# State-space block of a decoder: the read-outs of three pairs of states are added on GpSimd before TensorE sums them

## The reference, cut to what matters

```python
xz = x @ W_in                                   # x is the layer-normed input
x_in, z = jnp.split(xz, 2, axis=-1)
xc = silu(conv4(x_in) @ pw_kernel + conv_bias)
x_dbl = xc @ W_x                                # 16 delta ranks, 8 B, 8 C
delta = softplus(delta @ W_dt + b_dt)
deltaA = exp(delta * A)                         # per channel and state n
deltaB_u = delta * Bm * xc
def step(h, inp):
    dA_t, dBu_t, C_t = inp
    h = dA_t * h + dBu_t
    y_t = jnp.einsum('bn,bdn->bd', C_t, h)      # sum over the 8 states
    return (h, y_t)
y = y + xc * D
y = y * silu(z)
return y @ W_out
```

## Time and profile before

| | us |
|---|---|
| median of 3 runs | 3070.16 |
| the profiled execution, its own time | 3073.5 |
| its span, first to last instruction | 3071.7 |
| the 8 groups of this block, first scan to last finish (104.85 to 774.05) | 669.20 |
| one group in the middle of the block | about 85.0 |
| of it PE busy / DVE busy / ACT busy / POOL busy | 79.5 / 72.3 / 52.8 / 3.0 |

### The profile page before, as it was taken

One profiled execution on the slowest core, in us unless ns is written; L12 is line 12 of the kernel. 1 busy time (PEld: TensorE's weight loads), 2 busy tenths in 40 slices (PEclk: granted clock), 3 DMA queues, 4 the chain that ended last, 5 costly groups with the idle time before them and its releaser, 6 DMA issues. The chain is left out here.

```text
span 3071.7 us, 60127 instructions
## 1 busy us (share of the span) xinstructions
PE 2722.0 (89%) x20702; PEld 1767.6 (58%) x20703; DVE 1997.4 (65%) x4542; ACT 1518.1 (49%) x2982; POOL 454.4 (15%) x482
## 2 busy tenths in 40 slices
PE   6899999996799999999876689999999799969993
PEld 3344444443466676766665347777777645556662
DVE  2588888888367777777555447777777555653334
ACT  2666666663156666666443136666666233302222
POOL 0000000000300000000033111000110032324441
PEclk9899999997899999999877789999999899969997
DMA  4000000000100000000000100000000120001225
GB/s 112 0 1 0 0 0 0 0 0 0 35 21 20 20 15 20 20 20 15 1 15 1 39 11 26 20 20 20 20 25 11 49 83 20 14 26 61 63 61 165
DMA packets 57938, 80.70 MB, mean 26 GB/s; under 512 B 8880, under 2 KB 47059, under 8 KB 57491
## 3 DMA queue, kind: packets, MB, share of 16 engines
q1 hardware_dynamic: 51778, 62.69, 7.2%
q0 software_dynamic: 6048, 16.52, 1.7%
HBM read 63.59 MB, written 15.60 MB: 26 GB/s over the span
## 5 line engine op out<-in xcount | busy, mean ns | idle before, releaser
L1120 DVE CUSTOM_DVE_ANT_0 xa_h_scores<-xa_h_score_bank,xa_h_added 112x375 f32<-112x375 f32 x1024 | 518.1, 544 | 148.5 <-PE xa_h_score_bank L1055 133.6
L1214 ACT ACTIVATE xa_h_probs<-xa_h_scores,xa_h_negmax 112x375 f32<-112x375 f32 x1024 | 561.4, 600 | 0.9 <-DVE xa_h_negmax L1127 0.6
L1067 PEld LDWEIGHTS xa_h_turn_bank<-keep_ident,xa_h_probs 112*125 112x125 f32 x3072 | 398.6, 190 | 91.4 <-DVE xa_h_probs_t L1134 22.2
L1067 PE MATMUL xa_h_turn_bank<-keep_ident,xa_h_probs 112*125 112x112 f32 x3072 | 438.5, 279 | 8.8 <-DVE xa_h_probs_t L1134 8.5
L1134 DVE COPY xa_h_probs_t<-xa_h_turn_bank 125x448 f32<-125x448 f32 x512 | 319.1, 623 | 150.9 <-PE xa_h_turn_bank L1067 137.6
L1220 ACT ACTIVATE xa_h_probs_t<-xa_h_turn_bank 125x448 f32<-125x448 f32 x256 | 138.6, 541 | 304.5 <-PE xa_h_turn_bank L1067 304.5
L464 PE MATMUL mb_y_bank<-mb_read_out,keep_ident 128*128 128x448 f32 x512 | 231.7, 601 | 30.3 <-DVE mb_read_out L671 30.3
L664 DVE TENSOR_TENSOR_SCAN mb_state<-mb_decay,mb_drive 128x1792 f32<-128x1792 f32 x64 | 253.8, 3965 | 0.2 <-ACT mb_decay L598 0.2
L1055 PE MATMUL xa_h_score_bank<-xa_h_keys,xa_h_queries 32*112 32x375 f32 x2048 | 231.6, 522 | 11.3 <-DVE xa_h_row_max L1120 10.7
L1080 PEld LDWEIGHTS xa_h_sums_bank<-xa_h_probs_t,xa_h_values 125*32 125x32 f32 x6144 | 141.9, 110 | 154.5 <-DVE xa_h_probs_t L1134 149.2
L1080 PE MATMUL xa_h_sums_bank<-xa_h_probs_t,xa_h_values 125*32 125x112 f32 x6144 | 202.7, 265 | 14.6 <-issue 7.3
(11 more groups left out here) (341 smaller groups left out, 4145.7 us busy)
## 6 DMA issues: line engine op xcount, KB each, us to landing
xa_context<-in_ctx_t SPq DMA_DIRECT2D x64, 375.0 KB, 3.1
lm_w<-in_m_w SPq DMA_DIRECT2D x16, 512.0 KB, 9.9
lm_e_wide<-lm_result_rows SPq DMA_DIRECT2D x8, 896.0 KB, 9.8
keep_x<-in_x SPq DMA_DIRECT2D x4, 896.0 KB, 16.0
lm_latent_rows<-lm_rows SPq DMA_DIRECT2D x8, 448.0 KB, 3.2
out_x<-keep_x SPq DMA_DIRECT2D x8, 448.0 KB, 6.3
xa_mask_raw<-in_key_mask SPq DMA_DIRECT2D x1, 1312.5 KB
mb_f_pw<-in_pw SPq DMA_DIRECT2D x1, 1024.0 KB
```

Source lines behind the costliest of these rows:

```text
L1067: last = pe.transpose(turn_bank[(par + kc) % 2][0:KP, g * S:(g + 1) * S], probs[par][:, g, kc * KP:(kc + 1) * KP], keep.ident[0:S, 0:S])
L1120: dve.tensor_tensor_reduce(scores[par][:, g, :], score_bank[g][0:S, 0:SK], added[s][:, :], 1.0, -BIG, ALU.add, ALU.max, row_max[par][:, g: ...
L1214: act.activation(probs[par][:, g, :], scores[par][:, g, :], ACT.Exp, bias=negmax[s][:, G * c + g:G * c + g + 1]).then_inc(probs_ready, 1)
```

## The change

Three pairs of read-outs, of states 0 and 1, 2 and 3, 4 and 5, are added by POOL in SBUF (`add_pair`), and PE pushes the sum once, one state later (at n = 2, 4 and 6). States 6 and 7 are pushed singly as before. So a group has 5 pushes (20 matmuls) where it had 8 (32 matmuls), and 3 POOL additions of 128 x 1792 where it had none. The read-out tile has three buffers where it had two; `BUFFER` says in which one each state's read-out goes, `SUM` in which one POOL writes each sum (over one of its inputs). The read-outs of states 3, 5 and 7 now wait for POOL's additions, those of 4 and 6 for pushes. `skip` moves from state 0 to behind the first `convolve` in state 1. The pair additions stand ahead of `split_low` in POOL's queue.

```diff
--- before.py
+++ after.py
@@ -313,7 +313,7 @@
         delta, delta_inner = sb("delta", [128, IC, T]), sb("delta_inner", [128, IC, T])
         decay = sb("decay", [128, 2, IC, G, S])
         drive, state = sb("drive", [128, 2, IC, T]), sb("state", [128, 2, IC, T])
-        read_out = sb("read_out", [128, 2, IC, T])
+        read_out = sb("read_out", [128, 3, IC, T])
         gated_y = sb("gated_y", [128, IC, T])
         y_bank = [psum(f"y_bank{n}", [128, 512]) for n in range(IC)]
         front_bank = [psum(f"front_bank{n}", [128, 512]) for n in range(2)]
@@ -331,6 +331,11 @@
         decay_ready, drive_ready, state_ready, read_out_ready, summed = (
             sem(n) for n in ("decay_ready", "drive_ready", "state_ready", "read_out_ready", "summed"))
         skipped, gated, x_added = sem("skipped"), sem("gated"), sem("x_added")
+        pair_ready = sem("pair_ready")
+        PAIRS = 3
+        PUSHES = N - PAIRS
+        BUFFER = (0, 1, 2, 0, 1, 2, 0, 2)
+        SUM = (1, 0, 1)
         LOADED = mamba_w.count
 
         def slots(g):
@@ -381,7 +386,15 @@
                 pool.wait_ge(parts_cast, 2 * g + 2)
                 pool.tensor_tensor(low_parts[0:LOW, :], rest[0:LOW, :], low_parts[0:LOW, :], ALU.subtract).then_inc(split, 1)
 
+            def add_pair(g, k):
+
+                pool.wait_ge(read_out_ready, N * g + 2 * k + 2)
+                pool.tensor_tensor(read_out[:, SUM[k], :, :], read_out[:, BUFFER[2 * k], :, :], read_out[:, BUFFER[2 * k + 1], :, :],
+                                   ALU.add).then_inc(pair_ready, 1)
+
             def group(g, at, final=False):
+                for k in range(PAIRS):
+                    add_pair(g, k)
                 if not final:
                     split_low(g + 1)
 
@@ -458,11 +471,19 @@
                     last = pe.matmul(y_bank[c][:, 0:T], skip_diag[:, c, :], inner[:, c, :], start=True, stop=False)
                 last.then_inc(skipped, 1)
 
-            def add_state(g, n):
+            def push(held, stop):
+
+                for c in range(IC):
+                    last = pe.matmul(y_bank[c][:, 0:T], keep.ident[:, :], read_out[:, held, c, :], start=False, stop=stop)
+                last.then_inc(summed, 1)
+
+            def push_pair(g, k):
+                pe.wait_ge(pair_ready, PAIRS * g + k + 1)
+                push(SUM[k], False)
+
+            def push_state(g, n):
                 pe.wait_ge(read_out_ready, N * g + n + 1)
-                for c in range(IC):
-                    last = pe.matmul(y_bank[c][:, 0:T], keep.ident[:, :], read_out[:, n % 2, c, :], start=False, stop=n == N - 1)
-                last.then_inc(summed, 1)
+                push(BUFFER[n], n == N - 1)
 
             def project_out(g, half):
 
@@ -491,9 +512,10 @@
                         gate(g)
                         if not final:
                             turn_rows(g)
-                        skip(g)
                     if 1 <= n < 5 and not final:
                         convolve(g, n - 1)
+                    if n == 1:
+                        skip(g)
                     if n == 5:
                         if not final:
                             low_rank(g)
@@ -505,7 +527,10 @@
                             pe.wait_ge(split, 2 * (g + 2))
                             spread(g + 1, 0)
                         project_out(g, 1) if not first else pass_over(OUT_B)
-                    add_state(g, n)
+                    if n in (2, 4, 6):
+                        push_pair(g, n // 2 - 1)
+                    if n >= 2 * PAIRS:
+                        push_state(g, n)
 
             pe.wait_ge(loaded, LOADED)
             pe.wait_ge(setup, 1)
@@ -666,13 +691,16 @@
 
             def make_read_out(g, n):
                 dve.wait_ge(row_read[1], use_of_row(g, 1, n) + 1)
-                reuse(dve, summed, N * g + n - 1)
+                if n in (3, 5, 7):
+                    reuse(dve, pair_ready, PAIRS * g + n // 2)
+                else:
+                    reuse(dve, summed, PUSHES * g + {0: -1, 1: -2, 2: 0, 4: 1, 6: 2}[n])
                 dve.wait_ge(state_ready, N * g + n + 1)
-                dve.tensor_tensor(read_out[:, n % 2, :, :], state[:, n % 2, :, :],
+                dve.tensor_tensor(read_out[:, BUFFER[n], :, :], state[:, n % 2, :, :],
                                   rows[:, n % 2, 1, :].unsqueeze(1).broadcast_to([128, IC, T]), ALU.mult).then_inc(read_out_ready, 1)
 
             def finish(g):
-                dve.wait_ge(summed, N * (g + 1))
+                dve.wait_ge(summed, PUSHES * (g + 1))
                 dve.wait_ge(front_read[(GATES + 2) % 2], used(g, GATES + 2) + 1)
                 dve.wait_ge(front_read[(GATES + 3) % 2], used(g, GATES + 3) + 1)
                 for c in range(IC):
```

## The result

The changed kernel takes 3061.65 us (median of 9 executions, 3060.19 to 3069.17) against 3070.16 (9, 3064.97 to 3073.68) for the kernel before: ratio 0.9979, 95% interval 0.9970 to 0.9989. Run again on another occasion it gave 0.9977 (0.9966 to 0.9988). I had forecast 3073, a loss of 3 us that could not be told from none. The time lies in my range, but it went the other way, by just over the 0.2% that I had set as the bound.

A forecast was written before the change was run, and what follows sets the result against it. PE was taken to bound mid-group, with turn-taking at both ends. DVE's 568.4 us plus additions 92.4, cover -4.2, heads 6.4 + 4.4 and closing 5.0 gave a 672.4 us block, +3.2, hence 3073 us; range 3050 to 3100.

The forecast's parts named there:

- The bounds and the removal: Middle of a group: PE sets the pace at 9.4 us per state; three pushes fewer save it 9.0 us per group.
- the 1.64 us gaps: DVE's idle time before the drive of a next state, waiting for rows; forecast to go.
- The stall of DVE: Each POOL addition, 4.05 us, stops DVE for nearly its length: 3.85 us, 24 times, 92.4 us.
- The cover by `add_to_x`: Third addition runs beside `add_to_x` (input in PSUM), sparing DVE 0.6 us in seven groups, 4.2 in all.
- Rival 1: Additions cost DVE less than their length, 2.97 us each: 21 us less, 3052; chance 0.12.
- rival 2: POOL and DVE run side by side over long instructions, without blocking: 85 us less, 2985; chance 0.06.
- The heads: Group starts, where engines take turns: DVE's 3.58 us wait becomes 1.5 to 1.6 in four slow-gate groups, 6.4 us.
- The first group's wait: Head of the first group: DVE free at 116.4, rows at 120.8, so a wait of 4.4 us.
- The closing waits: End of the last group: DVE's waits for the last projection and last push, kept at 5.0 us.
- The sum for the block: All eight groups: DVE work, additions, cover, heads and closing waits give 672.4 us against 669.2, +3.2.
- Rival 3: PE at the lower clock makes rows late; drives of state 4 or 6 wait about 4 us: 3101; chance 0.20.
- The chances: Whole kernel against the one before: faster 0.27, same 0.34, slower 0.39.

The follow-up runs named there:

- half_additions: Changed kernel with each POOL addition over only the first two of four chunks (128x896 instead of 128x1792); ratio 0.9819 to the kernel before.
- after_padded: Changed kernel with 189 counting PE instructions ahead of PE's first wait for weights, restoring PE's old program length; ratio 1.0044 to the kernel before.
- after_again: Changed kernel run again with nothing altered; ratio 0.9977 to the kernel before, 3060.1 us in its profile.
- one_pair: Changed kernel with PAIRS = 1: only states 0 and 1 are added on POOL, 7 pushes a group; 3051.15 us, ratio 0.9936 to the kernel before.
- one_late_pair: Changed kernel with only states 4 and 5 added, pushed at state 6, and skip kept in state 0; ratio 0.9985 to the kernel before.
- memset_instead: Changed kernel with POOL filling the tile by a 128x1792 memset in place of each addition; ratio 0.9759 to the kernel before.
- No_additions: Changed kernel without the 24 POOL additions, each pair's push taking the second read-out alone; 3003.34 us, ratio 0.9772 to the kernel before.

## Why the prediction was wrong, and where it was right

**The bounds and the removal.** Right. PE set the pace in the middle, and the 1.64 us gaps went.

**The stall of DVE.** Right in mechanism and nearly in size: 3.71 us for 3.85, seen as drives of 5.74 us where I had said about 5.9. The half length gave half the stall (half_additions). The cover by `add_to_x` is right to the tenth, 3.71 - 3.11 = 0.6. Rival 1, the cheaper addition, is refuted by these rows, and rival 2 as well.

**The heads.** Mis-sized: I took 1.6 us per slow head, it is 2.6 (3.58 before), because PE's gates there run at the lower clock for 6.15 us where they took 4.97. The first group's wait is 4.2 for 4.4. The closing waits are 1.84 + 1.53 = 3.4, not 5.0. PE is busy 74.5 us in a middle group, where I had said 65 to 72, for the same reason: it runs the gates and some pushes at the lower clock.

**The sum for the block.** 672.4 forecast, 669.4 and 669.5 measured; a middle group 84.9 forecast, 85.3 measured. Against three profiles of the kernel before in which the block's code is its own (669.2, 665.6 and 665.6 with padding) the block is 0.2 to 3.9 us longer, which holds the forecast of +3.2. Part of that is luck, for the terms erred in both directions: the additions came 3 us cheaper (85 us for 88), the closing waits 1.6 shorter, the heads 4 dearer. And after_padded, with the same work, took 660.5. Rival 3 did not come: the second pair push of the third group does start late and at the lower clock (4.97 us), but the drives of states 4 and 6 never waited.

**The step that failed** is one I did not write as a step at all: that the block's change is the kernel's. I put the sum "on the profiled execution's 3073.5" as if the other 2300 us were fixed. They were not. The change moved PE's code, and with it a gap left the latent attention, 5 us, shown by padding either kernel. That term alone turns +3 into -2. In the two first profiles, whose spans differ by 6.9 us, it is nearly all: -0.4 us ahead of the block, +0.2 in it, -0.6 in the cross-attentions, -5.1 in the latent attention, -1.0 in the rest. The medians differ by 8.5 us and the ratio stands for 6.5. Beyond the 5 I find two things. One goes with the clock that the first cross-attention is granted: 6.8 us between two profiles of the changed kernel, in three stretches, 3.0 of it in the one at 0.88 or 0.62. The other is the 3 us that the changed kernel needs less behind that stretch in both profiles, without a known cause. If all nine of the shorter executions are like after_again, 6.4 us shorter behind the block, that is worth 9/16 x 6.4 = 3.6 us in the mean, and -2 becomes -5 to -6. That is an estimate: only one of the nine was profiled. What decides which clock is granted, and whether the change brings it about, stays open.

**The chances.** 0.27 on faster was low in the light of the result, but nothing in my rows priced the term that decided. That the time fell inside my range is owed to the range's width; its centre had the wrong sign.

## What to carry to other kernels

An addition moved to GpSimd is not free for VectorE where both read two SBUF inputs: price it as VectorE time of the addition's own length, and move only as much as VectorE's gaps will hold. Here one pair of three was right (3051 against 3062 and 3070). Where a forecast is a few us in 3000, pad the program of the old kernel to the new length before believing a gain: a change of nothing but code length was worth 5 us here. It is a test of what can move, not a correction, since two programs of one length (one_pair, one_late_pair) differed in the same gap. And when a cost is taken away, look at who gets the turn it leaves: without the additions POOL's split waited behind three DVE instructions, and the late softplus took back 28 us.

## What the runs showed of the hardware that I had not expected

- The place of PE's code decides about a gap of 3.5 to 4.3 us in a loop a long way behind the edit, and with it goes the number of fetch packets (71 with the gap, 61 or 62 without). Two programs 16,384 bytes apart behaved alike; two of equal length did not.
- 189 PE instructions that only count up a semaphore moved PE's first matmul from 12.35 to 32.10 us and the block by 20 us, though PE waits at that point anyway; 67 of them moved it to 13.62. Between the two that is 0.15 us each.
- Which engine gets its turn is not fixed. POOL's first split waits behind one DVE instruction in the earlier trace rows, 1.98 us in all. In memset_instead the same split, issued at 309.43, took 8.34 us: DVE's drive, read-out and scan all ran ahead of it, to 316.95, and it ran beside the statistics that start at 316.87. There the stall fell on POOL. No_additions has the same, 8.35 us.
- A POOL instruction that reads nothing (memset of 128x1792, 1.59 us) neither waits for a two-input scan nor slows it.
